# One-core transformer block: indirect dispatches sent one at a time, values projected once per tile, fills moved to SyncE

## The reference, cut to what matters

```python
x = x + attn(layernorm(x), Wqkv, Wout)        # 16 heads of 8, rotary q and k, each query sees itself and 63 keys before it
x = x + ffn(layernorm(x), ...)
# ffn: shared = silu(x@sg) * (x@su) @ sd
#      routing: top 4 of 8 groups, then top 4 of 32 experts, softmax gates; each expert takes 640 (token, choice) pairs
#      buf[e, pos] = x[token]                  # the scatter: "dispatch"
#      out_e = silu(buf@wg) * (buf@wu) @ wd ; result = shared + sum of gate * out_e[...]
```

## Time and profile before

| what | value |
|---|---|
| median of three runs | 875.8 us |
| the profiled execution | 876.49 us, of which 874.7 us is the span of its trace |
| mean granted TensorE clock | 0.807 of 2.4 GHz |
| start to the first strips on PE | 60 us |
| attention stage until the last dispatch | about 541.6 us |
| experts | 541.6 to about 832 us |
| gathering and adding | to 874.7 us |
| busy: PE, DVE, ACT, POOL | 659.7, 475.1, 285.9, 317.1 us |

### The profile page before, as it was taken

One profiled execution on the slowest core, in us unless ns is written; L12 is line 12 of the kernel. 1 busy time (PEld: TensorE's weight loads), 2 busy tenths in 40 slices (PEclk: granted clock), 3 DMA queues, 4 the chain that ended last, 5 costly groups with the idle time before them and its releaser, 6 DMA issues.

```text
span 874.7 us, 21218 instructions
## 1 busy us (share of the span) xinstructions
PE 659.7 (75%) x7569; PEld 531.6 (61%) x7569; DVE 475.1 (54%) x1508; ACT 285.9 (33%) x726; POOL 317.1 (36%) x335
## 2 busy tenths in 40 slices
PE   0146888787888788878787735989888898888891
PEld 0124666565666566656565523978878887788661
DVE  3246676665666566655664372644545454355178
ACT  0503442333323322332323321343434434343320
POOL 1200002324232423342323455255556565646600
PEclk9958896968677867776868558888998998988997
DMA  9955566443444343223310001333333343432076
GB/s 316 347 86 77 118 124 157 108 106 66 119 106 103 67 74 60 57 49 71 63 22 15 9 7 40 94 107 106 86 101 110 109 126 106 130 91 87 18 291 192
DMA packets 89835, 90.12 MB, mean 103 GB/s; under 512 B 12017, under 2 KB 71183, under 8 KB 89632
## 3 DMA queue, kind: packets, MB, share of 16 engines
q1 hardware_dynamic: 67312, 55.64, 27.8%
q10 hardware_dynamic: 13232, 21.44, 6.8%
q0 software_dynamic: 9216, 12.02, 4.9%
HBM read 49.62 MB, written 46.43 MB: 110 GB/s over the span
## 4 chain that ended last, share of the span: by engine, by line
PE 47%; another core or an unknown queue 14%; issue 12%; ACT 10%; DVE 5%; DMA 4%; ACTq 3%; SPq 2%; POOL 1%; DVEq 0%; POOLq 0%
PE bank L858 8%; PE bank L884 6%; PE bank L693 5%; PE bank L678 5%; ACT yout L594 3%; ACTq L476 3%; PE bank L625 2%; DMA kS<-rotated_parts 2%; PE bank L647 2%; PE bank L731 2%; ACT pt L494 2%; PE bank L789 2%; PE bank L633 2%; ACT hact L575 2%
## 5 line engine op out<-in xcount | busy, mean ns | idle before, releaser
L457 POOL DMA_INDIRECT pair_results<-yout,yidx x160 | 156.0, 975 | 135.1 <-ACT yout L594 94.4
L425 POOL DMA_INDIRECT expert_slots<-xfe,sidx x128 | 126.9, 992 | 140.4 <-DVE sidx L1090 81.9
L858 PE MATMUL bank<-xgT_parts,wgu_parts 128*128 128x320 f32 x768 | 152.6, 353 | 28.0 <-ACT hact L575 25.0
L858 PEld LDWEIGHTS bank<-xgT_parts,wgu_parts 128*128 128x128 f32 x768 | 130.4, 215 | 39.0 <-ACT hact L575 30.2
L1186 DVE TENSOR_TENSOR hact<-hact,bank 128x320 f32<-128x320 f32 x128 | 57.6, 483 | 133.7 <-ACT hact L575 124.1
L678 PE MATMUL bank<-pt,vals 128*32 128x64 f32 x2048 | 78.8, 245 | 60.3 <-issue 46.2
L678 PEld LDWEIGHTS bank<-pt,vals 128*32 128x32 f32 x2048 | 50.2, 122 | 85.4 <-issue 66.4
L494 ACT ACTIVATE pt<-bank 128x512 f32<-128x512 f32 x128 | 69.7, 596 | 88.0 <-PE bank L660 48.3
L934 DVE TENSOR_REDUCE mx<-bank 128x4 f32<-128x512 f32 x128 | 82.1, 683 | 28.1 <-PE bank L633 27.7
L884 PE MATMUL bank<-wdn,hact 128*128 128x128 f32 x640 | 84.5, 290 | 5.2 <-DVE hact L1186 3.2
L884 PEld LDWEIGHTS bank<-wdn,hact 128*128 128x128 f32 x640 | 84.0, 209 | 5.9 <-issue 5.9
(11 more groups left out here) (139 smaller groups left out, 1043.3 us busy)
## 6 DMA issues: line engine op xcount, KB each, us to landing
expert_slots<-fill ACTq DMA_DIRECT2D x4, 2600.0 KB, 24.7
xg<-expert_slots SPq DMA_DIRECT2D x32, 325.0 KB
pair_results<-zero ACTq DMA_DIRECT2D x8, 1024.0 KB, 5.0
rload<-pair_results SPq DMA_DIRECT2D x16, 512.0 KB, 5.4
rotated_parts<-parts SPq DMA_DIRECT2D x16, 384.0 KB, 4.9
qS<-rotated_parts SPq DMA_DIRECT2D x192, 32.0 KB
kS<-rotated_parts SPq DMA_DIRECT2D x144, 40.0 KB
wgu<-in_L_ffn_wg_dram SPq DMA_DIRECT2D x32, 128.0 KB
```

Source lines behind the costliest of these rows:

```text
L425: g.indirect_dma_start(out=slots_d, out_offset=bass.IndirectOffsetOnAxis(ap=sidx[:, z % NB, j, k:k + 1], axis=0), in_=xfe[:, z % NB, j, k, ...
L457: g.indirect_dma_start(out=pairs_d, out_offset=bass.IndirectOffsetOnAxis(ap=yidx[:, c, j:j + 1], axis=0), in_=yout[:, c, j, :], in_offset= ...
L858: last = mm(bank[2 + 2 * w + h][:, 0:CH], wgu_parts[:, e.b, wp, w, h * P:(h + 1) * P], xgT_parts[:, e.b, xp, ch * CH:(ch + 1) * CH], start ...
```

## The change

It does these things:

- **Dispatches one by one.** A tile's eight dispatches are spread over two steps (`y` is the tile one behind `z`), each behind a wait for something that DVE has done in that step (`paced`, `rope_sum`, `split_lo`); the pipeline has one more step.
- **Fills** are 32 DMAs of 325 KB that SP issues, eight at the start and eight behind the strip loads of each of tiles 0, 1 and 2; the zeros are 32 DMAs of 256 KB, four behind the loads of each of tiles 3 to 10.
- **Values.** Each tile's values are projected once (two matmuls); ACT makes the overlapping blocks with four copies, two of which move rows between the partition halves, the last from the previous tile's block in SBUF.
- **Weighted values back to rows** with eight plain transposes into two banks; DVE normalises in two halves.
- **Order.** On PE the output projection (L762) goes behind both calls of `weighted_values` and the third of `first_scores`. On ACT the exponentials go ahead of the copy `oT`. On DVE `maxima(1, 0)` and `rest` go ahead of the residual sum and its statistics, and `lengths` goes behind `minus`.

```diff
-    NZERO = 8
-    NFILL = 4
+    NZERO = NT
+    NFILL = NE
-            for tau in range(-1, NP + 6):
+            for tau in range(-1, NP + 7):
 # SyncE
+            def fill_slots(es):
+                for e in es:
+                    sp.dma_start(slots_v[e], fill[:, :, :].rearrange("p j c -> p (j c)")).then_inc(S.filled, 16)
+            sp.wait_ge(S.fill_done, 3)
+            fill_slots(range(8))
...
+                if m < 3:
+                    fill_slots(range(8 + 8 * m, 16 + 8 * m))
+                elif m < 11:
...
+                    zero_pairs(range(4 * (m - 3), 4 * (m - 2)))
 # GpSimd
+                y = z - 1 if z is not None else NP - 1 if n is None and f is None and r is None else None
+                def paced(maxima_done):
+                    if p is not None:
+                        pool.wait_ge(S.p1_reduced, NU * p + maxima_done)
+                        hold(pool)
+                if y is not None:
+                    dispatch(y, 1, 0)
...
+                if y is not None:
+                    paced(2)
+                    dispatch(y, 1, 1)
+                    paced(4)
+                    dispatch(y, 1, 2)
+                    if f is not None:
+                        pool.wait_ge(S.rope_sum, f + 1)
+                        hold(pool)
+                    dispatch(y, 1, 3)
...
-                    dispatch(0, range(TOPK))
-                    dispatch(1, range(1))
+                    paced(6)
+                    dispatch(z, 0, 0)
                 if w is not None:
                     pool.wait_ge(S.ln2, 8 * w + 8)
                     g.tensor_tensor(pout[:, w % 2], pin[:, :, :], mhalf[:, :].rearrange("p (a j) -> p a j", a=2), ALU.pow)\
                      .then_inc(S.w_pow, 1)
                 if z is not None:
-                    dispatch(1, range(1, TOPK))
+                    dispatch(z, 0, 1)
+                    paced(8)
+                    dispatch(z, 0, 2)
+                    if f is not None:
+                        pool.wait_ge(S.split_lo, f + 1)
+                        hold(pool)
+                    dispatch(z, 0, 3)
 # ScalarE
-            act.wait_ge(S.fill_done, 3)
-            per = NE // NFILL
-            for i in range(NFILL):
-                act.dma_start(slots_v[i * per:(i + 1) * per].rearrange("e p c -> p e c"),
...
-                    a.copy(vals[:, p % 2].rearrange("p j b h c -> p (j b) h c")[:, :, :, 0:DH],
-                           bank[4][:, :].rearrange("p (q h d) -> p q h d", q=4, h=H)).then_inc(S.v_evac, 1)
+                    a.copy(vals[:, b, :, 1, :, 0:DH], new).then_inc(S.v_evac, 1)
+                    a.copy(vals[WIN:P, b, :, 0, :, 0:DH], new[0:WIN]).then_inc(S.v_evac, 1)
+                    a.copy(vals[0:WIN, b, 1, 0, :, 0:DH], new[WIN:P, 0]).then_inc(S.v_evac, 1)
+                    if p:
+                        act.wait_ge(S.v_evac, 3 * p)
+                        a.copy(vals[0:WIN, b, 0, 0, :, 0:DH], vals[WIN:P, 1 - b, 1, 1, :, 0:DH]).then_inc(S.v_prev, 1)
 # TensorE
-                            at = (4 * j + q) * 4 * VW
-                            last = mm(bank[7][:, at:at + 4 * VW], pvT[:, j, q * P:(q + 1) * P], field("used"),
-                                      start=True, stop=True)
-                    last.then_inc(S.pvT_done, 1)
+                            last = nc.tensor.transpose(bank[7 - j][:, q * P:(q + 1) * P], pvT[:, j, q * P:(q + 1) * P],
+                                                       ident)
+                        last.then_inc(S.pvT_done, 1)
...
-                    for q in range(4):
-                        at = p * PW + q * WIN
-                        last = mm(bank[4][:, q * D:(q + 1) * D], xT_all[:, at:at + P], wqkv[:, 2 * D:3 * D],
+                    for j in range(2):
+                        at = WIN + p * PW + j * P
+                        last = mm(bank[4][:, j * D:(j + 1) * D], xT_all[:, at:at + P], wqkv[:, 2 * D:3 * D],
```

More of the change, by code:

```diff
@@ L32 @@
 NU = PW // P * H // 4
-VW = DH + 1
 NEG = -1e30
@@ L62, in constants @@
             head_rows[STRIP * s + part * NG:STRIP * s + (part + 1) * NG] = np.eye(NG)
-    used = np.zeros((P, 4 * VW), np.float32)
-    for i in range(4):
-        used[32 * i:32 * i + VW, VW * i:VW * (i + 1)] = np.eye(VW)
     fields = {
@@ L404, in step, with dispatch @@
             def step(n, f, p, s, w, r, z):
+                y = z - 1 if z is not None else NP - 1 if n is None and f is None and r is None else None
+                if z == 0:
+                    y = None
+                def dispatch(m, j, k):
+                    g.indirect_dma_start(
+                        out=slots_d, out_offset=bass.IndirectOffsetOnAxis(ap=sidx[:, m % NB, j, k:k + 1], axis=0),
+                        in_=xfe[:, m % NB, j, k, :], in_offset=None, bounds_check=NSLOT - 1,
+                        oob_is_err=False).then_inc(dispatched[m % NB], 16)
+                def paced(maxima_done):
[4 more added lines that the diff above has]
+                    dispatch(y, 1, 0)
                 if n is not None:
@@ L421, in step @@
                     g.memset(vals[:, :, :, :, :, DH:DH + 1], 1.0).then_inc(S.fills, 1)
-                def dispatch(j, choices):
-                    for k in choices:
-                        g.indirect_dma_start(
-                            out=slots_d, out_offset=bass.IndirectOffsetOnAxis(ap=sidx[:, z % NB, j, k:k + 1], axis=0),
-                            in_=xfe[:, z % NB, j, k, :], in_offset=None, bounds_check=NSLOT - 1,
-                            oob_is_err=False).then_inc(dispatched[z % NB], 16)
+                if y is not None:
[7 more added lines that the diff above has]
+                    dispatch(y, 1, 3)
                 if z is not None:
@@ L497, in values_out @@
                         act.wait_ge(S.pv_done, 2 * s + (j + 1))
-                        wait(act, S.pvT_done, s)
+                        wait(act, S.pvT_done, 2 * s - 1 + j)
                         a.copy(pvT[:, j], bank[6][:, :]).then_inc(S.pv_evac, 1)
@@ L508, in step @@
                         a.activation(ex4[:, j], ed4[:, j], ACT.Exp, accum_out=exs[:, j:j + 1]).then_inc(S.gate_exp, 1)
+                exponentials(0, 1)
                 if w is not None:
@@ L512, in step @@
                     a.copy(oT[:, :], bank[7][:, 0:PW]).then_inc(S.oT_evac, 1)
-                exponentials(0, 1)
                 if f is not None:
@@ L549, in step @@
                     a.copy(mT[:, :], bank[7][:, :].bitcast(BF16)[:, 0:PW]).then_inc(S.mT_evac, 1)
-                if f is not None and 3 <= f < 3 + NZERO:
-                    if f == 3:
-                        act.wait_ge(S.zero_done, 1)
-                    some = slice((f - 3) * NT // NZERO, (f - 2) * NT // NZERO)
-                    act.dma_start(pairs_v[some].rearrange("t p c -> p t c"),
-                                  zero[:, :].unsqueeze(1).broadcast_to([P, NT // NZERO, TOPK * D]))\
-                       .then_inc(S.zeroed, 16)
             attention_steps(step)
@@ L670, in weighted_values @@
                         wait(pe, S.pv_evac, 2 * s + j)
+                        wait(pe, S.onorm, 2 * s)
                     for i in range(0, 4, 2):
@@ L751, in step @@
                 if w is not None:
-                    pe.wait_ge(S.onorm, w + 1)
+                    pe.wait_ge(S.onorm, 2 * w + 2)
                     for j in range(2):
@@ L756, in step @@
                 if s is not None:
-                    pe.wait_ge(S.v_evac, s + 1)
+                    pe.wait_ge(S.v_evac, 3 * s + 3)
+                    wait(pe, S.v_prev, s)
                     weighted_values(0, 0)
+                    weighted_values(0, 1)
+                if p is not None:
+                    first_scores(1, 0)
                 if w is not None:
@@ L764, in step @@
                     last.then_inc(S.wout_done, 1)
-                if s is not None:
-                    weighted_values(0, 1)
-                if p is not None:
-                    first_scores(1, 0)
                 if r is not None:
@@ L1109, in step @@
                 at(f, rotate)
+                at(p, maxima, 1, 0)
+                at(f, rest)
                 at(w, add_attention)
                 at(w, second_stats)
-                at(p, maxima, 1, 0)
-                at(f, rest)
-                at(w, lengths)
                 at(r, scores)
@@ L1119, in step @@
                 at(p, minus)
+                at(w, lengths)
                 at(r, masked)
```

32 lines of the change are left out of this document (19 added, 13 removed).

## The result

The changed kernel took 813.65 us (median of 4 runs, 808.48 to 816.67) where the kernel before took 875.22 (median of 4, 872.47 to 875.92): a ratio of 0.930, 95% interval 0.924 to 0.935. The profiled execution has a span of 814.8 us against 874.7, 59.9 us less. Measured again later beside the kernel before at 874.73, it was 813.73 (ratio 0.929, 0.923 to 0.936). The later runs met four chips. One of them is as slow as this pair; the three others run the kernel before in about 712 us, and there the parts of the change and the full variants of the changed kernel that were timed gain 0.6% at most.

What follows compares the result with a forecast made beforehand. Back-to-back dispatches were taken to starve PE in steps, ACT's fills to bound the start, DVE the new step. 876.5 - 10 - 58 - 12 - 3 - 3 = 790.5, forecast 790 us, range 763 to 840.

Steps and rivals of the forecast that it cites:

- Start: Start of the kernel: ACT free of fills, first projection at 14.7 instead of 35.3; net -10 us, ends -20 and +3.
- the 10 us for the fills ahead of the strips: Tiles 1 to 4: fill groups queued on SP push the strips back by some 5 us, then 9 to 10.
- Ten full steps: Full tile steps from 132.4 to 423.7: from 29.1 us each to 23.3, 291.3 us to 233, -58.
- the run of four behind `pout`: Three dispatches behind `pout` and one heading the next step come almost as a run; 0.6 us a step.
- tight floor: Full step bound by in-order DVE: 20.1 us recorded work plus 0.3 for halves, floor 20.4 us; DVE at 85% or more.
- the shorter transposes, the values and the new order: PE savings in a step: transposes 0.9 to 1.7 us, values 0.8, counted at 0 beside DVE's chain.
- Two steps without new tiles: Two steps without `n` and `f`, 26.8 and 26.2 us, fall to 20.5 each: -12 us.
- Last step and tail: Step from 476.7: -3 us; end, where PE waits for `pout` behind one dispatch instead of five: -3.
- Experts and adding unchanged: Expert loop and adding part after the tile steps: no change in time.
- the fixed share of each dispatch: Rival: every dispatch costs its share wherever it stands; steps keep 6.5 us, 26.5 each, total 832 us; chance 0.2.
- The run that remains behind `pout`: Rival: run of four remains, fills fully exposed, strips or marks late by 2 us a step; 25.3 each, 822 us; chance 0.15.
- The slower case: Rival: dispatches keep their price, `pout` answers late; 3.3 us more in 13 steps, 889 us, decides over 30 us a step; chance 0.03.

Runs made afterwards that it cites:

- the spread version: Changed kernel with dispatches dealt out so none stand back to back behind `pout`, one behind it instead of three: 804.0 us, ratio 0.919 to the kernel before.
- fully spread: Changed kernel with dispatches dealt out and each expert's five result transfers also in single slots: 711.5 and 713.3 us, ratios 1.000 and 1.002 to the kernel before.

## Why the prediction was right, and where it was not

The forecast was 790 us, the run gave 813.65: inside the range, and faster as said, with the sum too good by 24 us. By its own steps, against the profiled span:

- **Start, forecast −10, measured −5.7** (the first scores that open the step at 132.44 in the earlier trace rows start at 126.75). ScalarE and the first projection came as said, at 6 us and at 14.42 where the forecast had 14.7. The term that was mis-sized is the 10 us for the fills ahead of the strips: of the 20.8 us by which the first projection comes earlier, 15 are gone by 126.75 and not 10, and TensorE still waits 10.2 us for the first `kS` at 39.23. The fills alone, elsewhere, gave 3.9 us.
- **Ten full steps, forecast −58, measured −51.6** (239.7 us against 291.3). The forecast gave the run of four behind `pout` 0.6 us; the steps came to 24.2 instead of 23.3, and with the run taken apart to 1.0 us less. The first of them, with no run in it, took 21.8. VectorE is no tight floor: its share in the step 246.8 to 271.2 is 75%, not the 85% that was to show. The 20.1 us that the floor was built on are those of one stretch, and more than a step's usual share; over the ten steps of before VectorE works 18.3 us a step.
- **The source of these 58.** The forecast put all of it on the runs and counted the shorter transposes, the values and the new order at nothing. The runs put back on the same chip divide it. From the fourth to the sixteenth copy to `mT` the kernel before takes 346.5 us in its first trace and 338.7 in its second, the changed kernel with runs 324.5, the changed one 288.1. So 36.4 us are the single slots and 14 to 22 the rest, by which trace of the kernel before is taken. The medians say the same of the whole: 36.9 us for the single slots and 24.1 for everything else, the start included. Counting that rest at zero was the step that failed, hidden by the runs' share being taken too large. Which of the three parts holds the 14 to 22 us was not separated. The end of VectorE's wait for the residual sum belongs to it: with the runs put back that wait is 9.1 us in all, against 73.3 before, so the new order removed it and not the single slots.
- **Two steps without new tiles, forecast −12, measured −4.5.** With fewer things to pace by, five dispatches stand back to back behind `pout`, 368.13 to 374.34, and the exponentials on scores that are ready at 371.37 start at 375.49.
- **Last step and tail, forecast −6, measured −1.3.** GpSimd waits 9.27 us for `pout`'s input at 436.69 with seven dispatches ready behind it, then sends 32 with one power between them. The dispatches that the changed kernel defers by a step come due here: 32 in the run where the earlier trace rows had 24. The sum had this as a gain. The table shows it once more, an end of 82 us with single slots and 77 with runs: TensorE's two early steps of the shared part stand under the run of 32 and take 25.5 us from their first matmul to the first expert's transpose (461.8 to 487.3), against 21.2 with the runs put back (496.3 to 517.5). That the run of 32 is what lengthens them is read from this coincidence, not tested.
- **Experts and adding unchanged: held.** From the first `yidx` on, the kernel before took 318.4 us and the changed kernel 317.5; in the second pair of traces 316.5 and 317.4. What the list leaves, 63.1 us listed against 59.9 measured, lies between the last dispatch and that `yidx`, 18.9 us instead of 14.7.

Of the rivals, the fixed share of each dispatch is refuted on the chip where it mattered, by 850.6 against 813.7 for the same 128 transfers. The run that remains behind `pout` is real and is a part, 1.0 us of a step by the spread version, not the 2 that its case had. The slower case needed steps over 30 us and did not come; no dispatch of the changed kernel lasts longer than 1.22 us. The forecast's figures rest on one chip's trace throughout. On three others the 6.5 us of a step that it meant to win back are not there: the kernel before with only the fills moved, its runs left in, has steps of 20.5 us. The changed kernel itself was not timed on them; the two variants of it that were and that keep all transfers, with runs and fully spread, are within 0.3% of the kernel before. That the gain hangs on the kind of chip was no part of the forecast, and its 790 us could only come true where the gaps exist.

## What to carry to other kernels

When "issue" gaps on TensorE and unnamed waits on ScalarE end just after a run of indexed transfers does, ask first whether another chip shows them: here the single slots were worth 37 us of 851 on one, and at most 0.6% (4 us) on three. Where they exist, deal the transfers out by semaphores that other engines raise anyway, but count where the deferred ones come due, and look at the slots behind every small operation that waits, since a run forms again there. And a part of a change that is counted at zero because another bound hides it should keep its own range; here it was 14 to 22 us.

## What the runs showed of the hardware that was not expected

The same kernel file differs far more from chip to chip than the change is worth. The kernel before took 874.7 us on one and 712.5, 712.6 and 710.7 on three others. Each of the four was met at one time only, so what belongs to the chip and what to that time is not separated; the slow figure came twice, in the first pair and again later. In the one kernel traced on both kinds, a step of the same code, from one tile's first dispatch to the next tile's, reads so on the 875 us chip and on a 712 us chip:

```profile
271.69:298.99 27.30, 19.72 (x352) 14.60 (x352) 18.33 (x70) 10.62 (x27) 9.73 (x10) 0.81 0.37 103
```

```profile
248.89:270.31 21.42, 15.59 (x352) 11.58 (x351) 18.27 (x70) 10.38 (x27) 9.65 (x11) 0.90 0.49 133
```

VectorE, ScalarE and GpSimd are busy for nearly the same time; TensorE is busy 4.1 us more and idles besides, at a granted clock of 0.81 against 0.90. In the expert loop the clock is 0.90 (575 to 675) against 1.00 (500 to 600). Whether the lower clock is a cause or only follows from the gaps, and what in a chip or beside it makes TensorE's issue gap under GpSimd's runs, no run here tells.
